# First layer: transform in even and odd frequencies, summed squares, merged expert matrices, first batch begun alone

## The reference, cut to what matters

```
xn = layernorm(x)                                  # (2, 512, 512), last axis
f = rfft(xn, axis=-1); corr = irfft(f * conj(f), n=512)
weights, delay = top_k(corr, 6); tmp = softmax(weights)
s = sum_k tmp_k * roll(xn, -delay_k)               # gather of 6 shifted rows
routing, _ = top_k(xn @ gate_w, 2)                 # 8 experts
shared = relu(xn @ up_w) ** 2 @ down_w             # 512 -> 1024 -> 512
routed = ((xn @ fc1_w) @ expert_w * sum(routing)) @ fc2_w   # 512 -> 256 -> 256 -> 512
x = x + s * silu(layernorm(shared + routed) * gamma + beta)
```

## Time and profile before

| what | us |
|---|---|
| median of three runs | 2103.69 |
| the profiled execution, whole | 2100.83 |
| its span, first to last instruction | 2098.8 |
| PE, DVE, ACT, POOL busy in the span | 1995.0, 1575.0, 1469.9, 1200.0 |
| first layer, to DVE's last statistics | 225.3 |

### The profile page before, as it was taken

How to read it: one execution, slowest core, us unless ns; L and a number is a source line. 1 busy time by engine, 2 the same in 40 slices (tenths; PEclk the granted TensorE clock), 3 DMA queues, 4 the chain that set the end, 5 groups by cost and what they waited for, 6 DMA issues and landing times.

```text
span 2098.8 us, 36800 instructions
## 1 busy us (share of the span) xinstructions
PE 1995.0 (95%) x10930; PEld 1587.3 (76%) x10930; DVE 1575.0 (75%) x2963; ACT 1469.9 (70%) x2933; POOL 1200.0 (57%) x823
## 2 busy tenths in 40 slices
PE   6999698989899999999999999999999999999986
PEld 5564466767788888888888888888888888888875
DVE  4546787875678787878778777878787878778776
ACT  3142675644778787877778787877787878778774
POOL 2514465753455656666566656655656565566655
PEclk9999799999999999999999999999999999999998
DMA  7404323243333333333233323333333333333433
GB/s 277 120 21 126 106 76 116 91 140 125 115 115 114 116 118 111 111 114 126 90 126 113 127 90 126 122 118 115 108 117 120 111 114 120 96 126 103 133 111 115
DMA packets 113840, 243.51 MB, mean 116 GB/s; under 512 B 23648, under 2 KB 24672, under 8 KB 112736
## 3 DMA queue, kind: packets, MB, share of 16 engines
q1 hardware_dynamic: 109792, 228.37, 32.5%
q0 software_dynamic: 3840, 12.59, 2.0%
HBM read 228.06 MB, written 12.85 MB: 115 GB/s over the span
## 4 chain that ended last, share of the span: by engine, by line
PE 74%; DVE 1%; issue 1%; ACT 1%; DMA 0%; SPq 0%; DVEq 0%; ACTq 0%
PE s_ps L71 13%; PE s_ps L73 12%; PE s_ps L72 12%; PE s_ps L1548 6%; PE s_ps_o L71 5%; PE s_ps_o L73 5%; PE s_ps_o L72 5%; PE s_ps L1518 5%; PE s_ps L1556 4%; PE s_ps L1510 3%; PE s_ps L1538 1%; PE s_ps L1496 1%; ACT s_lm L1628 0%; DMA s_wo_raw<-in_w_out 0%; PE s_ps L1502 0%
## 5 line engine op out<-in xcount | busy, mean ns | idle before, releaser
L1930 POOL TENSOR_TENSOR w_lo<-w_raw,w_hi 128x1024 fp32r<-128x1024 f32 x142 | 340.0, 2399 | 557.8 <-ACT w_hi L1610 557.8
L71 PE MATMUL s_ps<-h_hi,w_hi 128*128 128x512 f32 x1152 | 463.2, 402 | 9.1 <-DVE s_hid L1779 6.0
L73 PE MATMUL s_ps<-h_hi,w_lo 128*128 128x512 f32 x1152 | 451.0, 391 | 0.0
L72 PE MATMUL s_ps<-h_lo,w_hi 128*128 128x512 f32 x1152 | 450.0, 391 | 0.0
L1774 DVE SCALAR_TENSOR_TENSOR s_cv<-s_ps,s_par,s_cv 128x511 f32<-128x511 f32 (+2 forms) x480 | 355.8, 744 | 19.5 <-ACT s_cv L1653 13.7
L1947 POOL TENSOR_TENSOR s_lm<-s_lm,s_cbt 128x512 f32<-128x512 f32 x256 | 326.3, 1298 | 12.5 <-ACT s_lm L1635 12.5
L1628 ACT ACTIVATE s_lm<-s_rows,s_steps 128x128 f32<-128x128 f32 x1024 | 312.4, 390 | 2.2 <-PE s_ps L1548 2.2
L1653 ACT ACTIVATE s_cv<-s_ps,s_par 128x512 f32<-128x512 f32 x160 | 124.7, 779 | 238.9 <-PE s_ps L73 220.8
L71 PEld LDWEIGHTS s_ps<-h_hi,w_hi 128*128 128x128 f32 x1152 | 217.5, 189 | 54.5 <-DVE s_hid L1779 6.8
L73 PEld LDWEIGHTS s_ps<-h_hi,w_lo 128*128 128x128 f32 x1152 | 217.1, 188 | 47.0
L72 PEld LDWEIGHTS s_ps<-h_lo,w_hi 128*128 128x128 f32 x1152 | 217.8, 189 | 40.9
(11 more groups left out here) (232 smaller groups left out, 4078.8 us busy)
## 6 DMA issues: line engine op xcount, KB each, us to landing
w_raw<-in_w_in SPq DMA_DIRECT2D x144, 512.0 KB, 3.2
s_rows<-acs_dram SPq DMA_DIRECT2D x256, 256.0 KB, 4.3
s_wo_raw<-in_w_out SPq DMA_DIRECT2D x128, 256.0 KB, 3.7
w_raw<-in_gu_q SPq DMA_DIRECT2D x14, 512.0 KB, 3.3
f_d_q<-in_d_q SPq DMA_DIRECT2D x28, 256.0 KB, 2.6
f_d_w<-in_d_s SPq DMA_DIRECT2D x28, 256.0 KB, 3.5
table<-xn SPq DMA_DIRECT2D x16, 256.0 KB, 8.9
xs<-in_x SPq DMA_DIRECT2D x8, 256.0 KB, 4.3
```

Of the source, the lines that this page charges most:

```text
L71: nc.tensor.matmul(dst, l_hi, r_hi, start=start, stop=False)
L72: nc.tensor.matmul(dst, l_hi, r_lo, start=False, stop=False)
L73: return nc.tensor.matmul(dst, l_lo, r_hi, start=False, stop=stop)
L1930: nc.gpsimd.tensor_tensor(w_lo[:, slot, :], w_raw[:, slot, :], w_hi[:, slot, :].bitcast(F32), ALU.subtract).then_inc(w_lo_ready, 1)
```

## The change

The input tile is folded first: u = left half + right half, v = left half - right half (`pool_pairs` on POOL, scaled on DVE by `dve_uv`). Even frequencies depend on u alone, odd ones on v alone, so each transform block has two input blocks instead of four (`dft` has half as many columns). The weights gate, fc1 and up are folded alike (sum and difference of upper and lower half, times 0.5), on DVE, with their rounded copies on ACT. Cosine and sine powers of a frequency are added on POOL before the inverse transform, which has half the inputs and is done in three fp32r passes, with one more row (`nyq`) for the highest frequency. `expert_w` and `fc2_w` are multiplied once (`moe`, in batch 0), and the routed product takes `latT` directly. The start treats tiles 0 to 3; tiles 4 to 7 are loaded behind the up weights and transposed after the third block of the up projection. The table's rows `xn` are computed after all that, in the memory of the raw up weights. Batch n now runs transform, logits, latent, up, (expert product), inverse transform, shared and routed. On DVE, mixes 2 and 3 stand between output tiles.

```diff
...
+            for t in range(TB):
+                sp.dma_start(x1[:, t, :], x_view[:, t, :]).then_inc(x_loaded[t][0], 16)
             sp.dma_start(ident[:], a["ident"]).then_inc(ident_loaded, 16)
             sp.dma_start(dft, a["dft"]).then_inc(dft_loaded, 16)
...
+            sp.dma_start(fc1w, a["fc1_w"].rearrange("(k p) n -> p k n", p=P)).then_inc(small_loaded, 16)
+            sp.dma_start(gatew[:], a["gate_w"].rearrange("(k p) n -> p k n", p=P)).then_inc(small_loaded, 16)
+            for h in range(2):
+                c = slice(h * UP // 2, (h + 1) * UP // 2)
+                sp.dma_start(upw[:, :, c], up_view[:, :, c]).then_inc(up_loaded[h], 16)
+            for t in range(TB, NT):
+                sp.dma_start(x1[:, t, :], x_view[:, t, :]).then_inc(x_loaded[t][0], 16)
+            sp.dma_start(idft, a["idft"]).then_inc(rows_loaded, 16)
...
+            sp.dma_start(downw[:], a["down_w"].rearrange("(k p) n -> p k n", p=P)).then_inc(late_loaded, 16)
+            sp.wait_ge(table_lo_ready, 1)
+            sp.dma_start(expT, a["expert_w"].rearrange("(k p) n -> p k n", p=P)).then_inc(late_loaded, 16)
+            sp.wait_ge(split_lo_ready, 4)
+            sp.dma_start(fc2w, a["fc2_w"].rearrange("(k p) n -> p k n", p=P)).then_inc(late_loaded, 16)
...
+            for t in range(TB):
+                pe_turn(t, ps_a[:, t, :]).then_inc(pe_a, 1)
+            pe.wait_ge(table_lo_ready, 1)
             for n in range(NB):
                 cols = slice(n * SEQ, (n + 1) * SEQ)
 
-                pe.wait_ge(act_took, (n + 1) * TB)
+                if n:
+                    pe.wait_ge(dve_took, d_turn(NT - 1) + 1)
+                else:
+                    pe.wait_ge(xn_lo_ready, TB)
                 for m in range(KD):
                     i = a_dft(n, m)
                     turn(act_took, i)
-                    for k in range(KD):
-                        at = slice(m * P, (m + 1) * P)
+                    at = slice(m % 2 * P, (m % 2 + 1) * P)
+                    for k in (m // 2 * 2, m // 2 * 2 + 1):
                         mm = three_passes(nc, ps_a[:, i % 4, :], dft_hi[:, k, at], dft_lo[:, k, at],
-                                          xnT_hi[:, k, cols], xnT_lo[:, k, cols], k == 0, k == KD - 1)
+                                          xnT_hi[:, k, cols], xnT_lo[:, k, cols], k % 2 == 0, k % 2 == 1)
                     mm.then_inc(pe_a, 1)
...
+                pe.wait_ge(split_lo_ready, 4)
...
+                for m in range(KU):
+                    pe.wait_ge(split_lo_ready, KD + KD * (1 + 2 * m // KU))
+                    pe_up(n, m)
+                    if m == 0:
+                        pe_tok(n)
+                    if n == 0 and m == 2:
+                        for t in range(TB, NT):
+                            i = d_turn(t)
+                            turn(dve_took, i)
+                            pe_turn(t, ps_d[:, i % 4, :]).then_inc(pe_d, 1)
+                if n == 0:
+                    pe.wait_ge(late_loaded, 48)
+                    for m in range(KL):
+                        i = a_moe(m)
+                        turn(act_took, i)
+                        for k in range(KL):
+                            mm = nc.tensor.matmul(ps_a[:, i % 4, :], expT[:, k, m * P:(m + 1) * P], fc2w[:, k, :],
+                                                  start=(k == 0), stop=(k == KL - 1))
+                        mm.then_inc(pe_a, 1)
...
+                    i = d_corr(n, t)
+                    turn(dve_took, i)
+                    c = slice(t * P, (t + 1) * P)
+                    for j in range(2):
+                        three_passes(nc, ps_d[:, i % 4, :], pw_hi[:, j, c], pw_lo[:, j, c],
+                                     idft_hi[:, j, :], idft_lo[:, j, :], j == 0, False)
+                    nc.tensor.matmul(ps_d[:, i % 4, :], pn_hi[:, c], nyq[:], start=False, stop=False)
+                    nc.tensor.matmul(ps_d[:, i % 4, :], pn_lo[:, c], nyq[:], start=False,
+                                     stop=True).then_inc(pe_d, 1)
...
                     for k in range(KL):
-                        mm = nc.tensor.matmul(ps_a[:, j % 4, :], exoT[:, k, t * P:(t + 1) * P],
-                                              fc2w[:, k, :], start=(k == 0), stop=(k == KL - 1))
+                        mm = nc.tensor.matmul(ps_a[:, j % 4, :], latT[:, k, t * P:(t + 1) * P],
+                                              moe[:, k, :], start=(k == 0), stop=(k == KL - 1))
...
+                    if n == 0 and m == 0:
+                        act_up(1)
+                    if n == 0 and m == 2:
+                        for t in range(TB, NT):
+                            act.wait_ge(pe_d, d_turn(t) + 1)
+                            act_turned(t, ps_d[:, d_turn(t) % 4, :], late_hi_ready)
+                if n == 0:
+                    for m in range(KL):
+                        act.wait_ge(pe_a, a_moe(m) + 1)
+                        nc.scalar.activation(moe[:, m, :], ps_a[:, a_moe(m) % 4, :], ACT.Copy).then_inc(act_took, 1)
...
+            def dve_uv(t):
+                dve.wait_ge(sd_ready, t + 1)
+                nc.vector.tensor_scalar(uv[:, t, 0:D // 2], uv[:, t, 0:D // 2], mean2[:, t:t + 1], rstd[:, t:t + 1],
+                                        ALU.subtract, ALU.mult)
+                nc.vector.tensor_scalar(uv[:, t, D // 2:], uv[:, t, D // 2:], rstd[:, t:t + 1], None,
+                                        ALU.mult).then_inc(row_ready, 1)
...
+            def dve_up_pairs(h):
+                c = slice(h * UP // 2, (h + 1) * UP // 2)
+                dve.wait_ge(up_loaded[h], 16)
+                if h:
+                    dve.wait_ge(split_lo_ready, KD + KD)
+                else:
+                    dve.wait_ge(split_lo_ready, 4)
+                for j in range(2):
+                    nc.vector.tensor_tensor(pair[:, j, :], upw[:, j, c], upw[:, j + 2, c],
+                                            ALU.add).then_inc(pair_ready, 1)
+                for j in range(2):
+                    dve.wait_ge(pair_ready, KD + KD * h + j + 1)
+                    nc.vector.tensor_tensor(upw[:, j + 2, c], upw[:, j, c], upw[:, j + 2, c],
+                                            ALU.subtract).then_inc(pair_ready, 1)
...
+            for t in range(TB):
+                dve_stats(t)
+            dve_rstd(0)
+            for t in range(TB):
+                dve_uv(t)
+            for t in range(TB):
                 dve.wait_ge(act_took, t + 1)
...
+                dve_rest(t, ps_a[:, t, :]).then_inc(xn_lo_ready, 1)
+            dve.wait_ge(small_loaded, 32)
+            two = pair[:, 0, :].rearrange("p (k n) -> p k n", k=2)
+            eight = pair[:, 1, 0:2 * NE].rearrange("p (k n) -> p k n", k=2)
+            nc.vector.tensor_tensor(two, fc1w[:, 0:2, :], fc1w[:, 2:4, :], ALU.add).then_inc(pair_ready, 1)
...
+            tokens(0)
+            dve_up_lo(1)
+            for t in range(TB, NT):
+                dve.wait_ge(late_hi_ready, t - TB + 1)
+                dve_rest(t, ps_d[:, d_turn(t) % 4, :]).then_inc(dve_took, 1)
...
-                mix(n, 2)
-                mix(n, 3)
 
                 lag = 1 - n
                 for t in range(TB + 2 * lag):
                     g = n * TB + t
+                    if t in (1, 2):
+                        mix(n, t + 1)
...
+            def pool_pairs(t):
+                pool.wait_ge(*x_loaded[t])
+                nc.gpsimd.tensor_tensor(uv[:, t, 0:D // 2], x1[:, t, 0:D // 2], x1[:, t, D // 2:], ALU.add)
+                nc.gpsimd.tensor_tensor(uv[:, t, D // 2:], x1[:, t, 0:D // 2], x1[:, t, D // 2:],
+                                        ALU.subtract).then_inc(sd_ready, 1)
+            for t in range(TB):
+                pool_pairs(t)
+            pool.wait_ge(table_hi_ready, 1)
+            nc.gpsimd.tensor_tensor(dft_lo[:], dft, dft_hi[:].bitcast(F32), ALU.subtract).then_inc(table_lo_ready, 1)
+            for t in range(TB, NT):
+                pool_pairs(t)
             for n in range(NB):
+                for j in range(2):
+                    pool.wait_ge(act_took, a_dft(n, 2 * j + 1) + 1)
+                    nc.gpsimd.tensor_tensor(power[:, 2 * j, :], power[:, 2 * j, :], power[:, 2 * j + 1, :],
+                                            ALU.add).then_inc(power_ready, 1)
+                if n == 0:
+                    pool.wait_ge(table_hi_ready, 3)
+                    nc.gpsimd.tensor_tensor(idft_lo[:], idft, idft_hi[:].bitcast(F32),
+                                            ALU.subtract).then_inc(table_lo_ready, 1)
+                for j in range(2):
+                    pool.wait_ge(pw_hi_ready, 3 * n + j + 1)
+                    nc.gpsimd.tensor_tensor(pw_lo[:, j, :], power[:, 2 * j, :], pw_hi[:, j, :].bitcast(F32),
+                                            ALU.subtract).then_inc(power_ready, 1)
+                pool.wait_ge(pw_hi_ready, 3 * n + 3)
```

(31 more changed lines are left out.)

383 lines of the change are left out of this document (190 added, 193 removed).

## The result

| | before | after |
|---|---|---|
| median of seven runs, us | 2103.69 (2101.92 to 2108.17) | 2109.39 (2106.32 to 2112.0) |
| the profiled execution; its span | 2100.83; 2098.8 | 2109.39; 2107.4 |
| start of layer 2 on TensorE | 228.18 | 222.41 |
| from there to the end of the span | 1870.6 | 1885.0 |

The ratio is 1.0026, with a 95% interval of 1.0014 to 1.0038: the changed kernel is slower, if by little. The first layer is 5.8 us shorter, and the second, whose code nobody touched, 14.4 us longer.

What follows compares the result with a forecast made beforehand. TensorE was taken to bound the first layer until batch 1's top-k, then gathers and VectorE. Terms -8.9 + 16.8 - 7.4 - 7.0 = -6.5 took 2100.83 to 2094.3; with 2.86 for the median, 2097 us, range 2087 to 2104.

Steps and rivals of the forecast that it cites:

- A: First layer, start to first transform: 8.9 us shorter, the transform starting at 16.9 instead of 25.83.
- B: First layer, first transform to batch 0's first top-k: 16.8 us longer, 53.3 instead of 36.5.
- first rival: New GpSimd and VectorE operations don't hold each other: first layer ends near 208.9, total 2087; chance 0.20.
- C: First layer, batch 0's first top-k to batch 1's: 7.4 us shorter, 86.7 instead of 94.06.
- D: Batch 1's first top-k to the first layer's end: 7.0 us shorter, about 62 instead of 68.94.
- The sum: All four stretches of the first layer together: 6.5 us shorter, the layer ending at 218.8.
- second rival: First layer, the clock stays low longer after TensorE's waits: +6 us, 2103, no change; chance 0.10.
- third rival: First layer's gathers wait for a late table: +6 us, or 2109 if the queue is late too; chance 0.10.
- fourth rival: The earlier start of the first layer doesn't come: 5 us lost there, 2102; chance 0.10.

Runs made afterwards that it cites:

- after_3: The changed kernel as it is, run again in the second set: 2114.38 us, 1.0057 times the kernel before.
- after_pad101_3: The changed kernel with 101 idle TensorE instructions added behind the first layer, run again in the second set: 2098.92 us, 0.9974 times the kernel before.
- after_unroll_3: The changed kernel with the mixer's loop written out on all engines, run again in the second set: 2085.72 us, 0.992 times the kernel before.
- after_pad20: The changed kernel with 20 idle TensorE instructions added behind the first layer: 2131.49 us, 1.0131 times the kernel before.
- after_pad101: The changed kernel with 101 idle TensorE instructions added behind the first layer, first set: 2101.5 us, 0.986 times the kernel before.
- after_unroll: The changed kernel with the mixer's loop written out seven times on all engines, first set: 2086.06 us, 0.9793 times the kernel before.
- before_pad155: The kernel before with 155 idle TensorE instructions added behind the first layer, first set: 2144.43 us, 1.0071 times the kernel before.

## Why the prediction was wrong

The forecast was 2097, its range 2087 to 2104; 2109.39 lies outside. The step that failed is: "The second layer starts after a barrier and isn't changed, so whatever the first layer gains or loses goes to the total one to one." Its code isn't changed, but the place of its loop in TensorE's program is, and with that the loop takes 13.8 us more, a term that the sum had at nothing: shown by taking it away in the changed kernel (101, 40 and 216 instructions) and by giving it to the kernel before (155). None of my rivals had it; that the third one names 2109 is luck, for its cause, a late table, isn't there. The rows that could have warned stood in the trace before: six waits of TensorE on "issue", 6.5 us, in the loop.

The steps of the first layer, forecast and first trace:

- A, -8.9: it was -9.15. The held scaling and dft_lo took 2.43 each, and the first matmul came at 16.68 instead of 16.9.
- B, +16.8: +16.2. Its waits were 1.3 ahead of the up projection (forecast 3.7) and 4.4 ahead of the late transposes (forecast 2.2), in sum 5.7 for 5.9; the size of each was off, their order and cause (VectorE's remainders, its queue ahead of the tokens) were right. The first rival, no holding, is out. The held operations cost what the turns gave: 1.20 and 1.44 each on VectorE, 1.19 on GpSimd.
- C, -7.4: -6.0. The wait behind the logits was there, 7.1 us for 7.2, ended by ScalarE's square; each inverse tile took 2.2 (69.35, 71.50, 73.73, 75.96) where I had 1.8, as four of its eight matmuls, those around the two of one partition, start 0.31 to 0.34 apart instead of 0.227. (The terms of C as recorded add up to 156.6, not 156.9.)
- D, -7.0: -6.8, output tile 0 ahead of mix 2. (25.0 and 37.2 are 62.2, which is -6.7.)
- The sum, -6.5: -5.8 in the first trace. It isn't as firm as that looks: in after_3, after_pad101_3 and after_unroll_3 the second layer starts at 223.50, 224.47 and 225.93. Their first top-k is at 70.1, 70.6 and 72.0, and in the last two the granted clock of 40 to 60 us is 0.83 instead of the 0.91 of the first trace. My second rival, a clock that stays low longer, is partly true there. Between kernels with equal loops the gain is 3.7 us, where the sum had 6.5.
- The table's stores weren't waited for (third rival): the first gather follows the top-k by 2.8. The start came (fourth rival).

So with the loop at an equal place the measured ratio, 0.9974, lies inside the forecast range, by a little less gain than the 0.9968 forecast (2097 / 2103.69). The steps of the first layer came near one by one; that their sum did so well has some luck in it, as layer 2 starts anywhere from 222.41 to 225.93 in the four traces of the changed kernel named here.

## What to carry to other kernels

An edit ahead of a hardware loop moves the loop in each engine's program, and where its start lies shortly ahead of the end of a fetched piece (here 39 or 19 instructions ahead, with pieces of 256; with 79 no longer) each jump back stalls the engine twice. Read the waits on "issue" at the first operations of a loop before pricing an edit elsewhere, and compare two versions only with the loop at equal places, or written out. On an engine that bounds the loop, writing it out was worth 13.4 us in 1446.4, more than all that the change did to the first layer.

## What the runs showed of the hardware that was not expected

- Short stalls inside full work can take TensorE's clock to its lower level, 1.2 GHz. The granted clock of a stretch of 5 us is 0.50 behind jumps of the changed kernel and of after_pad20. It is low behind three of the changed kernel's six jumps (second stalls of 1.3 to 1.8 us), behind all six of after_pad20 (1.8 to 2.5), and behind none of the kernel before, where the longest stall is 1.6. The length of one stall does not tell: after_pad101_3 has the low clock behind its second jump (0.77 from 1032 to 1047), after a single stall of 1.7.
- Twenty instructions without any work cost 17 us, 0.8% of the kernel.
- In the first set the kernel before took 2129.6 us, 26 more than in the others, while after_pad101 took 2101.5 and after_unroll 2086.06, within 3 us of their times elsewhere. The trace of before_pad155 in that set has TensorE standing twice ahead of the expert product, once in each batch (waits from 60 to 200 us):

```profile
PE ps_a L283 <- issue: 20.7, 2, 10.8
```

  ScalarE got the first latent block 8.1 us after it had copied the logits, where the first trace of the kernel before has 2.8 (75.30 to 78.06), with the same matmuls issued at the same distance. The cause is open. The changed kernel, which computes the latent before the up projection and the expert product once, doesn't show it. Against the kernel before of that set, the changed one with the loop at the same place is 28 us faster; in the second set that difference is 3.7.
